# Two graph layers on one core: where the second layer's early gathers lie, and when four loads are asked for

## The reference

```
def gat_conv(h, src, dst, fc_w, attn_l, attn_r, bias, heads, out_feats):
    feat = (h @ fc_w.T).reshape(n, heads, out_feats)
    el = jnp.sum(feat * attn_l, axis=-1)
    er = jnp.sum(feat * attn_r, axis=-1)
    e = jax.nn.leaky_relu(el[src] + er[dst], 0.2)
    m = jax.ops.segment_max(e, dst, num_segments=n)
    ex = jnp.exp(e - m[dst])
    a = ex / jax.ops.segment_sum(ex, dst, num_segments=n)[dst]
    return jax.ops.segment_sum(feat[src] * a[..., None], dst, num_segments=n) + bias
...
h1 = relu(gat_conv(inputs, 8 heads) + norm * (inputs @ wb0.T + bb0))
h2 = gat_conv(h1, 1 head) + norm * (concat(inputs, h1) @ wb1.T + bb1)
x  = layernorm(inputs + h2)
...                     # then the third layer on x, with rel_w[edge_type], and two layer norms
```

## Time and profile before

| what | value |
|---|---|
| three runs | 2110.62, 2114.60 and 2114.86 us, median 2114.6 us |
| the profiled execution | 2110.05 us |
| its span, first to last instruction | 2108.0 us |
| busy | PE 1484.0 us (70%), DVE 1467.5 (70%), POOL 1322.2 (63%), ACT 530.3 (25%) |
| chain of work that ended last | POOL L885 36%, PE L1203 10%, "issue" 17%, DMA 10% |
| gathers of the second layer | 416, and 344 of them by L885 (ring) |

### The profile page before, as it was taken

How to read it: one execution, slowest core, us unless ns; L and a number is a source line. 1 busy time by engine, 2 the same in 40 slices (tenths; PEclk the granted TensorE clock), 3 DMA queues, 4 the chain that set the end, 5 groups by cost and what they waited for, 6 DMA issues and landing times.

```text
span 2108.0 us, 29310 instructions
## 1 busy us (share of the span) xinstructions
PE 1484.0 (70%) x7775; PEld 1132.6 (54%) x7776; DVE 1467.5 (70%) x2298; ACT 530.3 (25%) x886; POOL 1322.2 (63%) x1396
## 2 busy tenths in 40 slices
PE   6156666566786554886665697877776867489997
PEld 4134445455665544775554545655554545378874
DVE  5487788787786996775434483876767666777766
ACT  2000000000007991000000061544444444110127
POOL 1767777777702777577777605777777777135554
PEclk9567788778798556998778797988878887689999
DMA  5744444444406774344434428999999999868811
GB/s 160 167 116 128 128 125 129 128 125 130 110 14 205 218 210 122 99 130 123 120 115 120 120 110 290 304 339 336 346 341 339 339 334 351 296 242 288 295 58 61
DMA packets 234911, 406.17 MB, mean 193 GB/s; under 512 B 33200, under 2 KB 171622, under 8 KB 228198
## 3 DMA queue, kind: packets, MB, share of 16 engines
q0 software_dynamic: 73216, 219.89, 33.8%
q1 hardware_dynamic: 155701, 180.70, 26.8%
q10 hardware_dynamic: 5936, 4.95, 0.7%
HBM read 330.93 MB, written 74.48 MB: 192 GB/s over the span
## 4 chain that ended last, share of the span: by engine, by line
POOL 36%; PE 22%; issue 17%; DVE 11%; DMA 10%; ACT 2%; SPq 1%; DVEq 0%; ACTq 0%; POOLq 0%
POOL row_space L885 36%; PE ps L1203 10%; DMA row_space<-tab_kv,src_i 3%; DMA item_v<-row_space 3%; PE ps L1304 3%; PE ps L1426 2%; DMA arena<-rows_block_dst 2%; PE ps L970 1%; DVE arena L2512 1%; PE ps L1446 1%; DVE arena L2238 1%; DVE arena L1949 1%; ACT arena L1654 1%; DVE scores L2354 1%; PE ps L1228 1%
## 5 line engine op out<-in xcount | busy, mean ns | idle before, releaser
L885 POOL DMA_INDIRECT row_space<-tab_feat,src_i x760 | 728.9, 959 | 298.2 <-issue 230.5
L885 POOL DMA_INDIRECT row_space<-tab_kv,src_i x416 | 394.8, 949 | 197.9 <-issue 122.3
L1203 PE MATMUL ps<-arena 128*128 128x257 f32 (+1 forms) x1664 | 417.8, 412 | 122.0 <-DVE arena L2244 115.7
L1203 PEld LDWEIGHTS ps<-arena 128*128 128x128 f32 x1664 | 336.5, 206 | 196.6 <-issue 139.5
L1597 ACT COPY acc<-ps 128x265 f32<-128x265 f32 (+2 forms) x75 | 28.3, 377 | 1094.0 <-PE ps L1203 540.8
L1304 PE MATMUL ps<-arena 128*128 128x265 f32 x768 | 227.7, 460 | 96.4 <-DVE ps L2490 53.7
L1099 PE MATMUL ps<-acc,arena 128*128 x832 | 276.0, 489 | 0.0
L2238 DVE TENSOR_TENSOR arena<-row_space,ps 128x1280 f32<-128x1280 f32 (+1 forms) x94 | 174.3, 1854 | 140.4 <-DMA row_space<-tab_feat,src_i 138.6
L1304 PEld LDWEIGHTS ps<-arena 128*128 128x128 f32 x768 | 171.8, 229 | 142.0 <-issue 105.0
L2056 DVE TENSOR_TENSOR arena<-row_space,ps 128x1024 f32<-128x1024 f32 x104 | 126.8, 1219 | 136.2 <-PE ps L1099 73.9
L1099 PEld LDWEIGHTS ps<-acc,arena 128*128 128x128 f32 x832 | 190.0, 239 | 36.1
(11 more groups left out here) (387 smaller groups left out, 2266.1 us busy)
## 6 DMA issues: line engine op xcount, KB each, us to landing
item_v<-row_space SPq DMA_DIRECT2D x52, 1024.0 KB, 8.0
row_space<-item_v SPq DMA_DIRECT2D x52, 1024.0 KB, 5.0
arena<-rows_block_dst SPq DMA_DIRECT2D x104, 128.0 KB
row_space<-tab_feat,src_i POOLq DMA_INDIRECT x760, 2.8
scores<-rows_block_dst SPq DMA_DIRECT2D x52, 128.0 KB
arena<-rows_src_low SPq DMA_DIRECT2D x52, 128.0 KB
row_space<-tab_kv,src_i POOLq DMA_INDIRECT x416
arena<-rows_type SPq DMA_DIRECT2D x52, 128.0 KB
```

The source lines that it names most:

```text
L885: nc.gpsimd.indirect_dma_start(rows_of_slot(s)[:, g, :], None, table, bass.IndirectOffsetOnAxis(ap=src_i[:, item:item + 1], axis=0),).then ...
L1203: last = nc.tensor.matmul(ps[:, SUM_BANKS:2 * SUM_BANKS][:, bass.ds(bs[g], 1), 0:width].rearrange("p a d -> p (a d)"), onehot[:, s % 2, g, ...
```

## The change

Four things are done. `AHEAD` goes from 6 to 4 and the number of places behind the ring from 3 to 5, so that the total `EARLY` stays at 9: the ring's slots take groups 4 to 11 in place of 6 to 13, and two places in `base` take groups 12 and 13 in place of 4 and 5. The segment keys of `soft2` get a place in `scores`, and SP asks for them in `score2`, behind its first eight spreads, in place of at the start of `soft2`. The three small loads move from the start of `sum2` to the start of `node2`. SP's part of `soft2` keeps only its wait and its signal.

```
-AHEAD = 6
-EARLY = AHEAD + 3
+AHEAD = 4
+EARLY = AHEAD + 5
...
-        seg = [v[0].bitcast(I16), v[1], v[2].bitcast(BF16), v[3]]
+        seg = [scores[:, ITEMS * H2:ITEMS * H2 + SEG // 2].bitcast(I16), v[1], v[2].bitcast(BF16), v[3]]
...
+            def seg_rows(heads, chunks):
+
+                n = ITEMS // chunks * P
+                row = rows_d["dst"].rearrange("(c j) e -> c (j e)", c=chunks)
+                for h in range(heads):
+                    sp.dma_start(seg[0][h * chunks:(h + 1) * chunks, 0:n], row).then_inc(seg_in, 16)
...
                     for s in range(SLOTS):
                         spread_both(0, s, True)
+                    seg_rows(H2, ITEMS // 4)
                     with nc.sync.Fori(0, TURNS - 1) as u:
...
             begin(sp, "node2", ["dve", "pe", "act"])
             sp.dma_start(w_b[:], halves(a["wb1_t"][0:D, :])).then_inc(weights_in[1], 16)
             sp.dma_start(bias_all[:, 1, :], a["bb1"].broadcast_to([P, D])).then_inc(weights_in[1], 16)
+            sp.dma_start(bias_all[:, 0, :], a["bias2"].broadcast_to([P, D])).then_inc(weights_in[2], 16)
+            sp.dma_start(query_col[:], a["query"]).then_inc(weights_in[2], 16)
+            sp.dma_start(rel_sb[:], a["rel"]).then_inc(weights_in[2], 16)
...
             score_rows(1, "score2", "src_low")
-            seg_rows("soft2", H2, ITEMS // 4)
+            begin(sp, "soft2", ["dve", "pe", "act"])
+            end()
 
             begin(sp, "sum2", ["dve", "pe", "act"])
-            sp.dma_start(bias_all[:, 0, :], a["bias2"].broadcast_to([P, D])).then_inc(weights_in[2], 16)
-            sp.dma_start(query_col[:], a["query"]).then_inc(weights_in[2], 16)
-            sp.dma_start(rel_sb[:], a["rel"]).then_inc(weights_in[2], 16)
```

More of the change, by code:

```diff
@@ L652, in score_rows @@
                         keep(TURNS - 1, s)
[L653 to L661, removed]
                 end()
```

## The result

The changed kernel took 2101.9 us (median of 5 runs, 2098.98 to 2103.76) against 2114.6 (5 runs, 2110.62 to 2117.69): ratio 0.9948, 95% interval 0.9932 to 0.9964. Two later comparisons gave 0.9914 (0.9897 to 0.9932) and 0.9920 (0.9902 to 0.9937). The medians lie 12.7, 17.6 and 15.0 us apart; the forecast was 13.9 us, 2100.7. In the later two the changed kernel took 2092.4 and 2094.1 us, with before at 2110.0 and 2109.1, so the level itself moves by 5 to 9 us from the first comparison to the later ones.

A forecast was written before the change was run, and what follows sets the result against it. GpSimd's gathers in the second layer were taken to bound the kernel, with 17.10 us lost waiting for slot 0. The terms -16.8 + 1.5 + 1.2 + 0.2 = -13.9 us gave 2114.6 - 13.9 = 2100.7 us, range 2094 to 2106.

The forecast's parts named there:

- The bound: Second layer's gathers: an unbroken row but for 17.10 us, so a microsecond of GpSimd's wait is one of the kernel.
- Term 1: GpSimd's wait for slot 0 in `sum2`: 1.5 us left in place of 16.8, bounds nothing to 6.2.
- term 3: Keys' load among the spreads of `score2`: delays the release of slot 0 by 0.2 us, bounds 0 to 1.46.
- the 4.7 us: Sooner release of slot 0 by the moved loads: some 1.6 us at `soft2`'s scan, 3.1 at the start of `sum2`.
- The lower bound: No wait left at slot 0: with TensorE's full clock in `sum2`'s first group the release would be 1.95 us earlier.
- Term 2: Three load issues on SP at the start of `node2`: delay all gathers by 1.2 us, bounds nothing to 3.1.
- The bound "nothing": Start of `node2`: no cost if a store's issue, held 1612 ns, was held until a moment that stays.
- The sum: Whole kernel: -16.8 + 1.5 + 1.2 + 0.2 = -13.9 us, bounds -16.8 to -6.0; chance 0.78.
- The sums start no sooner: Rival, `sum2`: something other than the loads holds VectorE, 6.2 us of waiting stay; -9.2, 2105.4 us; chance 0.12.
- GpSimd issues slower beside VectorE: Rival, second layer: about 12 regained gathers slow down, 10.6 us lost again; -3.3, 2111.3 us; chance 0.06.
- SP's stores are held: Rival, `node2`: every store's issue held 1.08 us more, 54 us lost over 50 stores; some 2153 us; chance 0.04.
- A later stage that takes the gain back: Sign of being wrong, behind `sum2`: no place seen, since each stage from `node3` on starts from the previous one's end.

The follow-up runs named there:

- the kernel with the loads behind the scores: Changed kernel with the keys and three small loads asked for behind the last spread of `score2`: 0.9923, 2093.65 us; again 0.9918, 2093.61 us.
- the ring alone: Kernel before with only the two constants changed (AHEAD 4, EARLY = AHEAD + 5), loads unmoved: 0.9946, 2097.06 us; again 0.9938, 2096.05 us.
- The kernel with both edits: Changed kernel with the ring from group 3 and the keys and small loads behind `score2`'s last spread: 0.9910, 2089.77 us; again 0.9918, 2091.08 us.

## Why the prediction was right

**The bound.** It held that a microsecond of GpSimd's wait is one of the kernel. Over the three profiles of the changed kernel and the two of before, the wait fell from 16.89 to 2.04 on average (-14.85), and first to last gather from 538.48 to 522.64 (-15.84). The other 1.0 is 0.4 in the first 136 gathers and 0.6 in the 279 steps behind slot 0, not forecast and hardly above the scatter. With every order of the ring and every place of the loads it comes out so: in all 14 profiles the time from first to last gather, less the wait, is 519.0 to 521.9 us, while the wait goes from 0.3 to 17.1.

**Term 1, what is left.** Forecast 1.5 + 0.2 for term 3 = 1.7 us beyond the usual 0.30. Measured 2.98, 0.73 and 1.50, mean 1.74. That the mean meets the forecast so closely is luck in part, with 2.2 us between the three. Both parts of the 4.7 us came where they were said to: 1.61 at the scan (1.6 forecast), 2.92 at the start of the sums (3.1), in the first pair. What is late next was named rightly in both places, ScalarE's copy and its cleared bank.

The lower bound, no wait, was put down to TensorE's clock. The clock does move the wait, but the bound was not reached: the first 16 matmuls took 5.12 us or more in every profile, so none had the full clock from their start. Timeline of TensorE in `sum2` of the changed kernel, first group and third:

```profile
822.84 5.62 PE L1202 MATMUL ps<-arena 128*128 128x257 f32 x16 [6.21 <-DVE arena L2243]
...
830.47 3.63 PE L1202 MATMUL ps<-arena 128*128 128x257 f32 x16
```

and the stretches around it, columns as in the earlier trace rows:

```profile
822.00:826.00 4.00, 3.16 (x8) 2.52 (x8) 3.98 (x5) 0.00 (x0) 3.08 (x4) 0.50 0.43 121
826.00:828.00 2.00, 2.00 (x9) 1.74 (x8) 0.48 (x1) 0.00 (x0) 1.39 (x3) 0.82 0.34 107
828.00:830.00 2.00, 2.00 (x11) 1.76 (x10) 0.00 (x0) 0.00 (x0) 1.70 (x2) 1.00 0.38 115
```

The granted clock is 0.50 (1.2 GHz) as the group starts and 1.00 (2.4 GHz) as it ends. How long it stays at the low level moves the release. The two profiles of the kernel with the loads behind the scores show it, GpSimd at slot 0 and TensorE's first group, one execution:

```profile
818.30 5.12 PE L1202 MATMUL ps<-arena 128*128 128x257 f32 x16 [6.21 <-DVE arena L2243]
...
840.85 0.94 POOL L884 DMA_INDIRECT row_space<-tab_feat,src_i  x1 [1.56 <-DVE arena L2237]
```

and the other:

```profile
817.16 6.55 PE L1202 MATMUL ps<-arena 128*128 128x257 f32 x16 [6.21 <-DVE arena L2243]
...
841.13 0.95 POOL L884 DMA_INDIRECT row_space<-tab_feat,src_i  x1 [3.01 <-DVE arena L2237]
```

1.43 us more for the 16 matmuls, 1.45 more of waiting. The two numbers are so close by chance: the scores were also 0.48 later against the first gather, and GpSimd came to slot 0 0.45 later. The relation itself holds throughout: in all 14 profiles the multiplication of group 4 ends 20.91 to 20.92 us plus the time of these 16 matmuls after VectorE's first step of `sum2`. The changed kernel's first profile owes its 3.28 rather to late scores (127.41, against 125.61 where the wait was 1.03, though the 16 matmuls took 5.62 us with the longer wait and 6.00 with the shorter).

**Term 2, the three issues.** Forecast 1.2 us. The three profiles of the changed kernel have 35.10, 35.82 and 36.28 us from the start of `node2` to the first gather, before has 34.68 and 34.26: 1.26 more. Over all profiles it is 35.97 with the loads in `node2` (6 profiles, 35.10 to 36.38) and 34.37 without (8, 34.23 to 34.68): 1.60 more, and the two groups do not overlap. In the first pair the first store starts 2.49 us after the start of `node2` and not 1.18, so the three issues by themselves are 1.31, near the plain sum; the rest is the held issue, longer on average in the profiles with the loads. The bound "nothing" rested on the issue that was held; it was nearly right in the first profile alone (+0.42), where none was held. In the other five with the loads in `node2`, one issue was held as before, only earlier in the list, and the three issues then came on top. By the rule weighed there (the Trainium skill, DMA: Bandwidth & Descriptors, Issuing engines are not separate DMA queues, on the sequencer time as usually small) the term would have been nothing; 1.3 to 1.6 us between first gathers does not agree with that nothing. The issue is indeed small beside the transfer (0.43 us for `bias2` in the first profile, which landed 4.5 us after it was asked for), but here the issuing sequencer itself is late.

**Term 3, the keys among the spreads.** Forecast 0.2 within 0 to 1.46. Scores ready after 126.62 us with the keys there (5 profiles, 125.61 to 127.41) and 126.55 without (9, 126.02 to 127.84): 0.1, too small to tell from scatter. SP's pause behind the first eight spreads lasts 1.15 to 1.86 us without the keys and 1.18 to 1.95 with them, so it does hide most of the issue, as was said.

**The sum.** -15.8 + 1.3 = -14.5 by the traces in the stages that the sum names, -13.9 forecast, -12.7, -17.6 and -15.0 by the medians. The profiled executions as wholes differ by 11.5 only, as the untouched stages took 2.8 us more, on average, in the three of the changed kernel, and the step from the last gather to the attention 0.9. The difference was forecast with its mechanism; that 2101.9 lies so near 2100.7 is luck in part, since the same kernel took 2092.4 and 2094.1 later, below the range's 2094 and at it.

**The rivals.** *The sums start no sooner* would leave 6.2 us of waiting: that is the ring alone (6.06 and 7.49), not the changed kernel. *GpSimd issues slower beside VectorE*: the steps behind slot 0 stayed at 1.251 to 1.255 us in the three profiles, with the regained gathers among them. But the prediction was wrong to hold the even steps against the rule on two SBUF inputs: the large instructions of the sums read one of their two inputs from PSUM (`ps` in the earlier trace rows), and gathers beside instructions that read both from SBUF did become slower (last section). *SP's stores are held*: the longest was 0.62 us in the three profiles; the issues over 1 us were loads ahead of them. "A later stage that takes the gain back" was said to be absent; from the last gather to the attention's first it is 65.87 and 66.17 us before, 67.10, 66.62 and 67.15 after, some 0.9 us, which the runs do not separate from scatter.

## What to carry to other kernels

Where a queue waits on a ring's slot, ask which consumer step releases it, and let an earlier consumed group lie in the first reused slot; extra places that serve once belong behind it. A load that the consumer waits for is best issued where its queue has slack: the end of the loop that is already ahead (`score2`) cost nothing that shows, while the start of the stage whose queue was already late (`node2`) cost its issues in full. One pair of profiles had 6.9 us of differences in stages that the edit never touched; a second profile of each side is the cheapest way to see that.

## What was not expected of the hardware

**One held issue, at no fixed instruction.** In 13 of 14 profiles one of SP's first issues in `node2` takes some 0.3 to 1.3 us longer than its like, and which one differs. It is the `query` load in one execution of the changed kernel (0.43 elsewhere):

```profile
632.09 1.15 SPq L721 DMA_DIRECT2D query_col<-in_query  x1
```

the `bias2` load in another of the same kernel:

```profile
634.22 1.19 SPq L720 DMA_DIRECT2D bias_all<-in_bias  x1
```

and a store where the loads are gone (two of them, 0.95 to 1.10 when not held):

```profile
634.01 1.63 SPq L727 DMA_DIRECT2D hidden_t<-row_space  x2
```

In all 13 the held issue ends 1.8 to 2.8 us after the start of `node2`, whichever it is. So the prediction's thought of a hold until a moment that stays was not far off, but with the loads ahead it is a load that is held, and what follows it comes on top. What holds it was not tried and stays open.

**The same stage at either clock.** At the start of the attention the granted clock falls in some executions and not in others of one kernel. The ring alone, stretches of one execution and GpSimd's wait in them:

```profile
1289.00:1294.00 5.00, 2.54 (x13) 1.92 (x11) 1.63 (x4) 0.00 (x0) 3.78 (x5) 1.00 0.99 350
1294.00:1299.00 5.00, 5.00 (x18) 3.44 (x18) 0.00 (x0) 0.00 (x0) 3.78 (x5) 0.51 0.92 317
1299.00:1304.00 5.00, 5.00 (x18) 3.46 (x17) 2.50 (x3) 0.00 (x0) 0.31 (x1) 0.50 0.93 325
```

```profile
1305.49 0.95 POOL L885 DMA_INDIRECT row_space<-tab_kv,src_i  x1 [6.19 <-DVEq L1755]
```

and of another execution:

```profile
1288.00:1293.00 5.00, 2.56 (x14) 1.82 (x13) 1.27 (x3) 0.00 (x0) 3.78 (x5) 1.00 1.02 308
1293.00:1298.00 5.00, 5.00 (x28) 3.92 (x28) 2.41 (x2) 0.00 (x0) 3.78 (x5) 1.00 0.96 336
```

```profile
1299.92 0.94 POOL L885 DMA_INDIRECT row_space<-tab_kv,src_i  x1 [1.28 <-DVEq L1755]
```

TensorE was busy 2.5 of the 5 us ahead in both. With the clock at 0.50 it does 18 matmuls in 5 us, with 1.00 28, and GpSimd waits 4.9 us longer for the attention's first slot. In 11 of the 14 profiles the wait is 6.1 to 7.3 us, in the others 1.28, 2.09 and 4.25. The clock goes with it in every one: from TensorE's first matmul of the attention's items to that gather it stood at 1.2 GHz for 10.1 to 10.3 us in the 11, for 6.8 where the wait was 4.25, and not at all in the two others. One stretch of the execution with 2.09:

```profile
1288.00:1293.00 5.00, 4.71 (x27) 3.62 (x28) 1.50 (x2) 0.00 (x0) 3.78 (x5) 1.00 1.00 351
```

Why the clock falls in one execution and not in another stays open. The kernel with both edits, whose first comparison had runs at 2085.8 to 2087.0 and 2092.6 to 2095.4, has the waits of 2.09 and 4.25. That its two clumps are this clock fits the size but was not shown, as only one run of each comparison is profiled, and its second comparison (2089.99, 2091.08, 2091.08, 2095.17) has no two clumps. This scatter is larger than any of the small terms above.

**Which gathers are slow.** In all 14 profiles together, 60 of the second layer's 5824 gathers took over 0.97 us (up to 1.83). Every one of them overlaps an instruction of VectorE that reads two inputs from SBUF, as in the earlier trace rows the gather at 797.84 does the scan. Another, in the kernel before, beside a step on the residuals:

```profile
890.78 0.47 DVE L2251 SCALAR_TENSOR_TENSOR base<-bias_all,row_space 128x256 f32<-128x256 f32 x1
...
890.95 1.13 POOL L885 DMA_INDIRECT row_space<-tab_feat,src_i  x1 [0.30 <-issue]
```

Of the 3745 gathers that overlap two-input instructions with one input in PSUM, above all the sums' one-hot matrices and multiplications, and none with both in SBUF, not one took over 0.97 us. That the overlap itself is the cause was not tried, and 451 gathers with such an overlap were not slower.
